# A macaron block on one core: Gelu written back into PSUM, and the layer norms inside the attention applied by ScalarE from a scale and a shift that GpSimd makes

## The reference

```python
x = L0_attn_x                                     # (4, 1024, 128)
x = x + 0.5 * ffn(layernorm(x))
x = x + attention(layernorm(x))
x = x + 0.5 * ffn(layernorm(x))

# ffn(x): 8 experts, top 2 of a softmax gate, up 128->512, exact gelu, down 512->128
out = sum over e of sparse_w[..., e:e+1] * (gelu(x @ w_up[e].T) @ w_down[e].T)
return layernorm(out) + x
# attention: 16 heads of 64, causal linear attention on relu(Q), relu(K),
# both multiplied by cos and sin of the position; num / max(den, 1e-6); then @ Wo + bo
```

## Time and profile before

| | |
|---|---|
| median of 3 runs | 1236.83 us (1235.48 to 1241.78) |
| the profiled execution | 1232.84 us, of which the span of the core 1231.0 us |
| busy, of the span | PE 912.4 us, DVE 979.3, ACT 710.2, POOL 790.4 |
| setup, to the first pair | about 116 us |
| first expert stage, 46 pairs | about 116 to 283 us |
| attention, 64 steps | about 283 to 1034 us |
| second expert stage, 39 pairs | about 1038 to 1176 us |
| tail (gathering, last norm) | to 1231 us |

### The profile page before, as it was taken

How to read it: one execution, slowest core, us unless ns; L and a number is a source line. 1 busy time by engine, 2 the same in 40 slices (tenths; PEclk the granted TensorE clock), 3 DMA queues, 4 the chain that set the end, 5 groups by cost and what they waited for, 6 DMA issues and landing times.

```text
span 1231.0 us, 32392 instructions
## 1 busy us (share of the span) xinstructions
PE 912.4 (74%) x12594; PEld 741.2 (60%) x12594; DVE 979.3 (80%) x2124; ACT 710.2 (58%) x1033; POOL 790.4 (64%) x665
## 2 busy tenths in 40 slices
...
DMA packets 91778, 78.26 MB, mean 64 GB/s; under 512 B 7952, under 2 KB 81040, under 8 KB 91376
## 3 DMA queue, kind: packets, MB, share of 16 engines
...
q10 hardware_dynamic: 720, 0.23, 0.1%
...
## 4 chain that ended last, share of the span: by engine, by line
DVE 26%; POOL 26%; PE 24%; issue 14%; ACT 6%; DMA 3%; DVEq 0%; POOLq 0%; SPq 0%; ACTq 0%
POOL arena_a L1835 5%; DVE arena_b L1731 4%; POOL xs L784 4%; POOL arena_a L1817 4%; DVE arena_a L1689 3%; POOL xs L816 3%; PE bank L1493 3%; ACT arena_c L1605 3%; DVE arena_c L1727 2%; POOL arena_b L845 2%; PE bank L1417 2%; POOL arena_c L1839 2%; DVE xn_new L479 2%; PE bank L1419 2%; PE bank L1418 2%
## 5 line engine op out<-in xcount | busy, mean ns | idle before, releaser
L1835 POOL TENSOR_TENSOR arena_a<-arena_a 128x1024 f16<-128x1024 f32 x64 | 139.1, 2173 | 52.4 <-ACT arena_a L1605 51.5
L1817 POOL TENSOR_TENSOR arena_a<-arena_b,trig_rows 128x512 f32<-128x512 f32 x128 | 160.4, 1274 | 6.8 <-issue 6.8
L1605 ACT ACTIVATE arena_c<-arena_a 128x1024 f16<-128x1024 f32 x64 | 67.6, 1057 | 164.6 <-DVE arena_a L1689 164.6
L1714 DVE TENSOR_TENSOR arena_b<-bank,decay 128x512 f32<-128x512 f32 x128 | 82.4, 686 | 47.6 <-PE bank L1493 47.1
L1605 ACT ACTIVATE arena_b<-arena_b 128x512 f16<-128x512 f32 x128 | 78.3, 629 | 64.8 <-DVE arena_b L1714 64.8
L1332 POOL DMA_INDIRECT ys<-arena_b,row_at x78 | 85.2, 1092 | 35.8 <-issue 22.3
L997 ACT ACTIVATE arena_c<-bank,s_pre 128x1024 f32<-128x1024 f32 x46 | 51.2, 1114 | 94.9 <-PE bank L932 89.8
L1417 PE MATMUL bank<-wo_hi,arena_c 128*128 128x128 f16 x256 | 53.1, 238 | 69.9 <-DVE arena_c L1698 69.9
L816 POOL DMA_INDIRECT xs<-xhl,slot_idx x64 | 78.6, 1228 | 40.4 <-issue 40.4
L1838 POOL TENSOR_TENSOR arena_c<-arena_c 128x130 f16<-128x130 f32 x64 | 29.7, 464 | 111.3 <-ACT arena_c L1655 111.3
L1689 DVE SCALAR_TENSOR_TENSOR arena_a<-bank,trig_cols 128x512 f32<-128x512 f32 x128 | 82.4, 684 | 23.3 <-PE bank L1419 23.0
...
## 6 DMA issues: line engine op xcount, KB each, us to landing
...
```

Source lines behind the costliest of these rows:

```text
L1605: nc.scalar.activation(dst, src, ACT.Copy, scale=scale).then_inc(done, 1)
L1714: i = nc.vector.tensor_tensor(probs[:, h * BLK:(h + 1) * BLK].rearrange("p (c i) -> p c i", c=TPB), ps_so[:, h, :].rearrange("p (c i) -> p ...
L1817: i = nc.gpsimd.tensor_tensor(q_trig[h], q_relu[h], trig_rows[:, bass.ds(u * BLK, BLK)], ALU.mult)
L1835: nc.gpsimd.tensor_tensor(q_lo, arena_a[:, 0:2 * BLK], q_hi, ALU.subtract).then_inc(a["q_lo_done"], 1)
```

## The change

1. `h32` is no longer an SBUF buffer; it is a view of `ps_pre`. The Gelu reads and writes the same PSUM place, `h_hi` and `h_lo` are both made from there, the Gelu's wait for `low(p-2)` is gone, and `up(p)` on TensorE waits for `low(p-2)` in place of the Gelu of p-2. This holds for both expert stages.
2. `(var + eps) * 4` moves from VectorE (L465, L878) to GpSimd in all `ln_stats` and `combine`; GpSimd also makes a shift, minus mean times the root, so `ln_power` and `finish_power` have four instructions instead of one.
3. In the attention, `ln_apply` of hp 2 and hp 6 and the first half of `finish_apply` of hp 3 leave VectorE. ScalarE applies them (`ln_line`, `finish_line`) as Identity with scale and shift: at the end of hp 2 `ln_line(1, n-1)` and, for n = 1 to 4, `finish_line`; at the end of hp 5 `ln_line(0, n+3)`. The addition to `x_tok` moves from hp 3 to hp 4, ahead of the statistics. In the expert stages `ln_apply` and `finish_apply` stay with VectorE.

```diff
-        h32 = [take(PAIR * BLK) for _ in range(2)]
+        h32 = [ps[:, :, :].rearrange("p c t -> p (c t)") for ps in ps_pre]
...
         def ln_power(g, r, n):
-            g.wait_ge(ln_var, turn(r, n) + 1)
-            nc.gpsimd.tensor_tensor(rstdh[:], var4[:], minus_half[:, 0:TPB], ALU.pow).then_inc(ln_rstd, 1)
+            g.wait_ge(ln_mean, turn(r, n) + 1)
+            nc.gpsimd.tensor_scalar(var4[:], mv[:, :, 1], LN_EPS, 4.0, ALU.add, ALU.mult).then_inc(ln_step, 1)
+            at_least(g, ln_norm, turn(r, n))
+            g.wait_ge(ln_step, 2 * turn(r, n) + 1)
+            nc.gpsimd.tensor_tensor(rstdh[:], var4[:], minus_half[:, 0:TPB], ALU.pow)
+            nc.gpsimd.tensor_scalar(ln_shift[:], mv[:, :, 0], -1.0, None, ALU.mult).then_inc(ln_step, 1)
+            g.wait_ge(ln_step, 2 * turn(r, n) + 2)
+            nc.gpsimd.tensor_tensor(ln_shift[:], ln_shift[:], rstdh[:], ALU.mult).then_inc(ln_rstd, 1)
+
+        def ln_line(act, r, n):
+            act.wait_ge(ln_rstd, turn(r, n) + 1)
+            act.wait_ge(ln_tr, turn(r, n))
+            r_was, n_was = LN_ORDER[turn(r, n) - 1]
+            if r_was:
+                act.wait_ge(f["x_sum"], 2 + n_was + 1)
+                act.wait_ge(xhl_lo, 2 + n_was + 1)
+            for t in range(TPB):
+                i = nc.scalar.activation(xn_new[:, t, :], tile_of(x_tok, n, t), ACT.Identity, bias=ln_shift[:, t:t + 1],
+                                         scale=rstdh[:, t:t + 1])
+            i.then_inc(ln_norm, 1)
...
+        def finish_line(act, q):
+            act.wait_ge(f["fin_rstd"], q + 1)
+            for t in range(TPB):
+                i = nc.scalar.activation(zt[:, t, :], zt[:, t, :], ACT.Identity, bias=fin_shift[:, t:t + 1],
+                                         scale=frstdh[:, t:t + 1])
+            i.then_inc(f["fin_z"], 1)
...
             def up(G, at_e):
                 pe.wait_ge(f["x_copied"], G + 1)
                 if G > 1:
-                    pe.wait_ge(f["gelu_done"], G - 1)
+                    pe.wait_ge(f["lo_done"], G - 1)
...
                         act.wait_ge(f["up_done"], G + 1)
-                        if G > 1:
-                            act.wait_ge(f["lo_done"], G - 1)
-                        nc.scalar.activation(h32[G % 2], ps_pre[G % 2][:, :, :].rearrange("p c t -> p (c t)"), ACT.Gelu,
+                        nc.scalar.activation(h32[G % 2], h32[G % 2], ACT.Gelu,
                                              scale=s_pre[:, 0:1]).then_inc(f["gelu_done"], 1)
```

More of the change, by code:

```diff
@@ L309, in build @@
         arena_free = sem("arena_free")
-        ln_read, ln_mean, ln_var, ln_rstd, ln_norm = (sem(f"ln_{n}") for n in "read mean var rstd norm".split())
+        ln_read, ln_mean, ln_step, ln_rstd, ln_norm = (sem(f"ln_{n}") for n in "read mean step rstd norm".split())
         ln_tr, ln_hi, ln_lo = (sem(n) for n in ("ln_tr", "ln_hi", "ln_lo"))
@@ L849, in finish_power @@
         def finish_power(g, q):
-            g.wait_ge(f["fin_var"], q + 1)
-            nc.gpsimd.tensor_tensor(frstdh[:], fvar4[:], minus_half[:, 0:TPB], ALU.pow).then_inc(f["fin_rstd"], 1)
+            g.wait_ge(f["fin_ag"], q + 1)
+            nc.gpsimd.tensor_scalar(fvar4[:], fmv[:, :, 1], LN_EPS, 4.0, ALU.add, ALU.mult).then_inc(f["fin_step"], 1)
+            at_least(g, f["fin_z"], q)
+            g.wait_ge(f["fin_step"], 2 * q + 1)
+            nc.gpsimd.tensor_tensor(frstdh[:], fvar4[:], minus_half[:, 0:TPB], ALU.pow)
+            nc.gpsimd.tensor_scalar(fin_shift[:], fmv[:, :, 0], -1.0, None, ALU.mult).then_inc(f["fin_step"], 1)
+            g.wait_ge(f["fin_step"], 2 * q + 2)
+            nc.gpsimd.tensor_tensor(fin_shift[:], fin_shift[:], frstdh[:], ALU.mult).then_inc(f["fin_rstd"], 1)
+        def finish_line(act, q):
[4 more added lines that the diff above has]
+            i.then_inc(f["fin_z"], 1)
         def combine(v, q):
@@ L876, in combine @@
             i.then_inc(f["fin_ag"], 1)
-            v.wait_ge(f["fin_ag"], q + 1)
-            nc.vector.tensor_scalar(fvar4[:], fmv[:, :, 1], LN_EPS, 4.0, ALU.add, ALU.mult).then_inc(f["fin_var"], 1)
         def finish_apply(v, q):
             tiles = slice((q % 8) * TPB, (q % 8 + 1) * TPB)
-            v.wait_ge(f["fin_rstd"], q + 1)
-            for t in range(TPB):
-                i = nc.vector.tensor_scalar(zt[:, t, :], zt[:, t, :], fmv[:, t, 0:1], frstdh[:, t:t + 1],
-                                            ALU.subtract, ALU.mult)
-            i.then_inc(f["fin_z"], 1)
+            if q < EARLY:
+                v.wait_ge(f["fin_rstd"], q + 1)
+                for t in range(TPB):
+                    i = nc.vector.tensor_scalar(zt[:, t, :], zt[:, t, :], fmv[:, t, 0:1], frstdh[:, t:t + 1],
+                                                ALU.subtract, ALU.mult)
+                i.then_inc(f["fin_z"], 1)
             v.wait_ge(f["fin_z"], q + 1)
@@ L1665, in attention_act @@
                         ahead(n, hp, lambda to: v_low(to, s + 1))
+                        if hp == 2:
+                            if n > 0:
+                                ln_line(act, 1, n - 1)
+                            if 0 < n <= EARLY:
+                                finish_line(act, EARLY + n - 1)
+                        if hp == 5:
+                            if 0 < n <= EARLY:
+                                ln_line(act, 0, EARLY + n - 1)
                         if n == 4 and hp == 6:
@@ L1765, in beside @@
                         combine(v, late)
[L1766 removed]
+                    if hp == 4:
                         finish_apply(v, late)
[L1768 removed]
                         v.wait_ge(f["fin_x"], late + 1)
                         ln_stats(v, 0, late)
[L1771 to L1772 removed]
                 if 1 < n <= EARLY + 1 and hp == 0:
```

16 lines of the change are left out of this document (5 added, 11 removed).

## The result

The changed kernel takes 1218.78 us in the median of four runs (1214.61 to 1220.65), the one before 1237.76 us on the same chip (1235.48 to 1241.78): a ratio of 0.985, 95% interval [0.983, 0.988]. The forecast was 1215.5 us. The total came out near the forecast, but by luck: two of its three stages did not come out near theirs, and their errors have opposite signs.

A forecast was written before the change was run, and what follows sets the result against it. No engine was full in the attention; a loop of waits bounds it. Terms -5.8 + 2.7 + 0.5 - 10.3 - 8.4 = -21.3 on the profiled 1232.84 gave 1211.5, plus 4.0 for the median 1215.5 us; range 1205 to 1231.

The forecast's parts named there:

- low during first_sum: First expert stage: low parts beside GpSimd's L394 no longer held up once h32 is in PSUM, -5.8 us.
- start of each stage: Start of both expert stages: down(0) comes 1.4 us later, after up(2), never made up; twice, +2.7 us.
- undisturbed pairs: Expert stages, some 60 of 85 pairs: `up` waiting for low(p-2) costs nothing; pairs stay at 2.87 us.
- hp 1: Attention step hp 1, blocks 1 to 3: L465 leaves VectorE, -0.95 us each; no such gain in block 4.
- hp 3: Attention step hp 3, blocks 1 to 3: 11.7 us instead of 13.72, ScalarE 2.5 us beyond its hole; -2.0 each.
- hp 4: Attention step hp 4, blocks 1 to 3: L890 is new there, less L465's 0.17 us; +1.0 us each.
- hp 6: Attention step hp 6, blocks 1 to 3: the third L479 goes, 0.5 us of ScalarE's activations remains; -1.1 us each.
- hp 2: Attention step hp 2, blocks 1 to 3: L479's 1.61 us goes, 1.2 charged for GpSimd being 1.4 later; -0.4 each.
- Block 6, -3.5 at hp 1: Attention block 6: L465, which took 5.44 us waiting out GpSimd's operations, is gone; 3.5 us of 5.3 taken as gain.
- GpSimd shuts VectorE out at new places: Rival: L1731 held up at hp 2 or hp 5, 11 places, up to 5.3 us each; four or more, chance 0.05.
- -18.7: Attention, first to last step: the forecast's terms for this stage make it 18.7 us shorter.
- VectorE the cheaper place (0.02): Rival: the moved sets cost VectorE 1.11 us undisturbed, ScalarE 1.65, so moving them loses: 1245 us, chance 0.02.

The follow-up runs named there:

- e9: e7 with GpSimd's scatters of block 6, hp 1 and hp 3, issued in later steps: 1183.7 us, ratio 0.957 to the kernel before.
- e2: The kernel before with the Gelu's result in PSUM in the second expert stage only: 1218.7 us, ratio 0.985.
- e5: The changed kernel with one more SBUF addition on VectorE per pair, behind the low part in the second expert stage: 1222.6 us, ratio 0.992 to the kernel before.
- e6: The changed kernel with finish_power and the gather of hp 1 moved to GpSimd's idle time in hp 0: 1200.9 us, ratio 0.974 to the kernel before.
- e7: e6 with the addition of the combined rows to x moved back from hp 4 to hp 3: 1195.6 us, ratio 0.969 to the kernel before.
- e8: e1 with finish_power and the gather of hp 1 moved to hp 0 as in e6, normalizations on VectorE: 1210.6 us, ratio 0.983.
- e1: The kernel before with only the Gelu's result moved into PSUM and `up` waiting for the low part: 1215.9 us, ratio 0.983.

## Why the prediction was right in the sum, and where it was wrong

- **low during first_sum, -5.8; start of each stage, +2.7; undisturbed pairs.** Right: -5.8, and pairs at 2.87 us. `up(2)` itself starts 2.2 us later in the first stage (122.78 against 120.62) and 2.0 in the second (23.3 instead of 21.3 us behind the last step's start); the work behind it is later by less, `up(3)` by 1.4 us (125.66 against 124.30) and 1.5 (27.1 instead of 25.6), which is the 1.4 forecast. (Twice half of 2.87 is 2.9; the 2.7 of the sum is a slip of no weight.) The in-place Gelu costs nothing: low(16) ends at 168.07, 0.69 us ahead of `up(18)` (0.62 before), and a Gelu of the second stage takes 1.09 us in place against 1.11.
- **hp 1, hp 3, hp 4, hp 6.** Right within 1.1 us in blocks 1 to 4, but for block 4's hp 6 (9.3 us where the terms make 10.9). ScalarE does delay hp 3, as forecast; that it also delays hp 4 did not appear (hp 4 grows by VectorE's L923 and statistics).
- **hp 2, the step that failed.** "GpSimd is now 1.4 us later (two chains at 0.7)". It is 4.0 us later. The forecast added the durations of undisturbed small operations; the rows show what it left out: the root 2.07 us instead of 1.05, beside VectorE's L1732 (483.41 to 484.63) with two SBUF operands, a scale of 0.75 instead of 0.20, beside L1769 (487.43 to 488.65), 0.65 us ahead of the gather, and hand-overs of 0.15 and 0.46. The forecast charged 1.2 us for GpSimd on a step of 9.21; the step took 14.68, so GpSimd's lateness cost 5.5 us, for 5.2 us against the step's start. That nearly every late microsecond counts was right; how many there would be was not. Four blocks together: 14.0 instead of -1.6 us.
- **Block 6, -3.5 at hp 1.** It came out as -2.8, but the next step lost 5.3 us as an L1769 of 6.7 us: the rival "GpSimd shuts VectorE out at new places", at one of its eleven places. The same L1769 takes 6.7 to 6.9 us in every run with ScalarE's normalizations but e9, and 1.22 in every run with VectorE's. The errors of hp 2 and of block 6, +15.6 and +5.3, with 4.2 us of slips in block 0, turn -18.7 into about +6; measured +5.0.
- **What no term had.** The low part of the second stage, out of SBUF, also frees GpSimd's scatters: 12 to 13 us (e2), and by e5 it is VectorE's two SBUF operands that hold them up. The forecast weighed only what GpSimd does to VectorE there, and not the reverse. It had seen in the attention and beside `first_sum` how the two engines meet, and did not ask it of the second stage.
- **VectorE the cheaper place (0.02).** Ruled out by e6 and e7 against e8. As the change stood, though, the place was worth nothing either way: e1 gains 20.8 us on the kernel before, the changed kernel 19.0 and 21.1.
